# Final attention scores handed over bank by bank in two of five attention stages, in a kernel without staging copies and with reordered transposes

## Time and profile before

| | |
|---|---|
| median of 3 runs | 1514.12 us (1513.02 to 1522.76) |
| the profiled execution, its own time | 1511.47 us |
| its span, first to last instruction | 1509.8 us |
| PE busy | 1293.7 us (86%) |
| PEld busy | 855.9 us (57%) |
| DVE busy | 953.6 us (63%) |
| ACT busy | 610.6 us (40%) |
| POOL busy | 336.1 us (22%) |
| mean granted PE clock | 0.916 |

### The profile page before, as it was taken

One profiled execution on the slowest core, in us unless ns is written; L12 is line 12 of the kernel. 1 busy time (PEld: TensorE's weight loads), 2 busy tenths in 40 slices (PEclk: granted clock), 3 DMA queues, 4 the chain that ended last, 5 costly groups with the idle time before them and its releaser, 6 DMA issues. The chain is left out here.

```text
span 1509.8 us, 37147 instructions
## 1 busy us (share of the span) xinstructions
PE 1293.7 (86%) x13707; PEld 855.9 (57%) x13707; DVE 953.6 (63%) x2842; ACT 610.6 (40%) x1343; POOL 336.1 (22%) x1014
## 2 busy tenths in 40 slices
PE   3888887837858887997998887899999958999998
PEld 3777765624536773443666775435788844444443
DVE  5777737876456766998336876624777754555454
ACT  3666644651236662222344554642444421111111
POOL 1222210220033430000113331423565550000000
PEclk9999997967968997999999998756999988999999
DMA  9400000000000000000000000001000000000000
GB/s 288 104 3 3 3 2 1 2 1 1 2 1 2 3 3 1 1 1 1 1 1 2 3 3 2 1 1 57 3 3 3 3 1 0 8 15 7 7 7 15
DMA packets 26393, 21.14 MB, mean 14 GB/s; under 512 B 5936, under 2 KB 22640, under 8 KB 26224
## 3 DMA queue, kind: packets, MB, share of 16 engines
q1 hardware_dynamic: 25216, 18.67, 4.4%
q10 hardware_dynamic: 1008, 0.16, 0.1%
HBM read 16.74 MB, written 2.10 MB: 12 GB/s over the span
## 5 line engine op out<-in xcount | busy, mean ns | idle before, releaser
L311 DVE TENSOR_REDUCE neg_max<-ps 128x8 f32<-128x1024 f32 (+1 forms) x264 | 253.9, 962 | 167.6 <-PE ps L570 163.8
L559 PE MATMUL ps<-qTm,kT 32*128 32x512 f32 (+1 forms) x1056 | 247.7, 543 | 28.0 <-DVE neg_max L311 15.0
L570 PE MATMUL ps<-kT,qTm 32*128 32x128 f32 x3200 | 242.7, 287 | 0.2 <-DVE kT L332 0.2
L570 PEld LDWEIGHTS ps<-kT,qTm 32*128 32x128 f32 x3200 | 218.8, 199 | 6.2 <-issue 3.6
L476 ACT ACTIVATE probs<-ps,bias_col 128x512 f32<-128x512 f32 (+1 forms) x192 | 159.2, 829 | 123.3 <-PE ps L578 123.3
L674 PE MATMUL ps<-probs,v_wide 128*32 128x128 f32 x3200 | 116.2, 278 | 33.1 <-DVE o_sb L350 28.3
L1734 PE MATMUL ps<-kv_all,ctx_all 128*128 128x512 f32 x256 | 134.1, 606 | 5.2 <-DVE kv_all L1648 5.2
L559 PEld LDWEIGHTS ps<-qTm,kT 32*128 32x128 f32 x1056 | 83.9, 187 | 88.2 <-issue 44.9
L1672 ACT ACTIVATE kv_all<-ps,b_col 128x512 f32<-128x512 f32 x64 | 44.0, 687 | 218.8 <-PE ps L1712 218.8
L1712 PE MATMUL ps<-q_all,ctx_all 128*128 128x512 f32 x256 | 132.4, 600 | 0.0
L1648 DVE TENSOR_SCALAR kv_all<-ps,b_col 128x512 f32<-128x512 f32 x64 | 48.0, 750 | 116.5 <-PE ps L1712 116.5
(11 more groups left out here) (371 smaller groups left out, 2562.3 us busy)
## 6 DMA issues: line engine op xcount, KB each, us to landing
ctx_all<-in_ctx SPq DMA_DIRECT2D x4, 1024.0 KB, 10.5
x_all<-in_x SPq DMA_DIRECT2D x4, 512.0 KB, 6.7
out<-x_all SPq DMA_DIRECT2D x8, 256.0 KB, 2.3
ctx_all<-in_W1T SPq DMA_DIRECT2D x1, 1024.0 KB, 5.1
tap_w<-in_conv_wT SPq DMA_DIRECT2D x1, 768.0 KB
w_l<-in_w SPq DMA_DIRECT2D x2, 256.0 KB
rope<-in_c_rope SPq DMA_DIRECT2D x1, 256.0 KB
cls_mask<-in_amask SPq DMA_DIRECT2D x1, 256.0 KB
```

Source lines behind the costliest of these rows:

```text
L311: nc.vector.tensor_reduce(neg_max[:, k, H2 * u:H2 * u + H2].rearrange("p (a h) -> p a h", a=2), ps[:, 4 * u:4 * u + 2, 0:N].rearrange("p a ...
L559: nc.tensor.matmul(score_bank(g), kT[rows_of(g), k, :], qTm[rows_of(g), k, 0:N], start=not masked_scores, stop=False, skip_group_check=True)
L570: last = nc.tensor.matmul(pair_of(u, g)[:, 128 * i:128 * i + 128], qTm[rows_of(g), k, 128 * i:128 * i + 128], kT[rows_of(g), k, :], start= ...
```

## The change

In all attention stages:

- The copies `key32` and (in `post` stages) `row32` go; PE transposes from `ctx_all`, `kv_all`, `q_all` or `qk_tiles` directly.
- In `turns`, the part that signals `last_turned` comes first. In `post` stages it still holds the transpose of the maxima (bank 7) and the pick of the outputs; in the others (L0, L2: `raw`) the transpose of the maxima moves to bank 6 and to the end of the part that signals `first_turned`.
- DVE's `take_o` moves from behind `take_oT` to right behind the maximum of half 0. In raw stages it no longer waits for `nmT_ready`; there `take_qT` does.
- A half's final scores are handed over by bank in L2 and L3 (`BANKS`: 'banks'), with two semaphore counts for each half, and two exponentials of 256 columns in place of one of 512. L0, L1 and L4 stay with 'pairs'. (The third kind, 'ring', is written but no stage uses it.)

Elsewhere: the de-pooling stage gets two banks each for `ends` and `counts`, one bank for the turned rows, and PE's order becomes `ends`, `counts`, `matrix`, `turn`, `total`. The cross stage loses POOL's copy. In the experts' stage POOL waits before each of its 8 adds for `mo_choice` of that group.

```
+        BANKS = {'L0': 'pairs', 'L1': 'pairs', 'L2': 'banks', 'L3': 'banks', 'L4': 'pairs'}
+        def final_jobs(L):
+            return 2 if BANKS[L] == "pairs" else 4
+        def final_bank(L, b, g):
+            return 3 + (4 * b + (g + 2) % 4) % 3 if BANKS[L] == "ring" else 2 + g % 2
...
             def take_qT(b, k):
                 dve.wait_ge(*after("first_turned", b + 1))
+                if not post:
+                    if b < 2:
+                        dve.wait_ge(*after("early_nmT", b + 1))
+                    else:
+                        done(dve, "nmT_ready", b - 2, count)
...
                 dve.wait_ge(*after("last_turned", b + 6))
-                done(dve, "nmT_ready", b + 3, count)
+                if post:
+                    done(dve, "nmT_ready", b + 3, count)
...
                 at(2, take_max, 0)
+                at(6, take_o)
                 at(1, take_qT)
                 at(1, take_kT)
                 if post:
                     at(7, take_oT)
-                at(6, take_o)
...
             def exps(b, k, u):
+                if final_jobs(L) == 4:
+                    for g in (2 * u, 2 * u + 1):
+                        act.wait_ge(*after("scores", b * 4 + (g + 2) % 4 + 1))
+                        nc.scalar.activation(probs[:, k % 2, N * g:N * (g + 1)], ps[:, final_bank(L, b, g), 0:N],
+                                             ACT.Exp, bias=bias).then_inc(sem("probs_ready"), 1)
+                    return
...
+            def final_free(b, g):
+                if final_jobs(L) == 4:
+                    job, held = 4 * b + (g + 2) % 4, 3 if BANKS[L] == "ring" else 2
+                    if job >= held:
+                        pe.wait_ge(*after("probs_ready", job - held + 1))
...
+                    for g in s_groups:
+                        final_free(b, g)
+                        dst = ps[:, final_bank(L, b, g), 0:N]
...
+                        nc.tensor.matmul(dst, kT[rows_of(g), k, :], qTm[rows_of(g), k, 0:N],
                                          start=not masked_scores, stop=False, skip_group_check=True)
...
+                def turn_max(last):
+                    if item(3):
+                        done(pe, "nm_split", item(3)[0], count)
+                    slot = item(3)[1] if item(3) else (at_one - 2) % RING
+                    return nc.tensor.transpose(turned_max(post), nm3[:, slot, :], identb[:])
+                max_read()
+                done(pe, "o_scaled", at_one - 6, count)
+                done(pe, "pv_ready", at_one - 5, count)
+                last = turn_max(None) if post else None
+                if item(6):
...
+                    nc.tensor.transpose(ps[:, 6, 0:128], query_rows(b, k), ident[:])
+                    last = nc.tensor.transpose(ps[:, 6, 128:256], key_rows(b), ident[:])
+                if raw:
+                    last = turn_max(last)
...
+        def ends_bank(b):
+            return 4 + 3 * (b % 2)
+        def counts_bank(b):
+            return 5 - 4 * (b % 2)
...
-                wait_reuse(pe, after("dp_bound"), b, 1)
+                wait_reuse(pe, after("dp_bound"), b, 2)
...
-            steps(pe, B, [(4, matrix), (4, turn_rows(pe)), (5, total), (2, counts), (0, ends)])
+            steps(pe, B, [(0, ends), (2, counts), (4, matrix), (4, turn), (5, total)])
...
                 rows = x_all[:, bass.ts(i, 4), :]
+                pool.wait_ge(sem("mo_choice"), i + 1)
                 nc.gpsimd.tensor_tensor(rows, rows, z_all[:, bass.ts(i, 4), :], ALU.add).then_inc(sem("mo_joined"), 1)
```

More of the change, by code:

```diff
@@ L593, in mask_whole @@
             def mask_whole(b, k):
[L595 to L596 removed]
                 for a in range(2):
+                    raw_free(b, 2 + a)
                     for part in range(mask_parts):
[L599 removed]
+                        nc.tensor.matmul(ps[:, raw_bank(L, b, 2 + a), 0:N], identb[:], mask(k, part).unsqueeze(1).broadcast_to(four),
                                          start=part == 0, stop=False, skip_group_check=True)
@@ L610, in turns, with max_read @@
                 at_one = ahead[1][0] + ahead[0] - 1
+                def max_read():
+                    done(pe, "nmT_ready", at_one - 3, count)
+                    if L in BIASES and at_one in (1, 2):
+                        pe.wait_ge(*after("early_nmT", at_one))
+                early = L in BIASES and at_one < 2
+                def turn_max(last):
+                    if not (item(3) or early):
+                        return last
+                    if L in BIASES and item(1):
+                        done(pe, "bias_set", item(1)[0], count)
+                    if item(3):
[7 more added lines that the diff above has]
+                if item(6):
+                    b, k = item(6)
+                    for half in range(2):
+                        last = nc.tensor.matmul(ps[:, 7, 256 + W * half:256 + W * half + W],
+                                                pv[:, k % 2, 128 * half:128 * half + 128],
+                                                pv_pick[:, 0 if heads == 16 else 1, 0:W], start=True, stop=True)
+                if last is None:
+                    pe.sem_inc(sem("last_turned"), 1)
+                else:
+                    last.then_inc(sem("last_turned"), 1)
                 done(pe, "q_masked", at_one - 1, count)
@@ L665, in weighted @@
                 done(pe, "pv_ready", b - 1, count)
-                done(pe, "nmT_ready", b + 2, count)
+                if post:
+                    done(pe, "nmT_ready", b + 2, count)
                 done(pe, "o_scaled", b - 1, count)
@@ L669, in weighted @@
                 for half in (1, 0):
-                    pe.wait_ge(*after(ready, b * 2 + (2 - half)))
+                    each = 1 if cut_later else final_jobs(L) // 2
+                    pe.wait_ge(*after(ready, (b * 2 + (2 - half)) * each))
                     for i in range(deep):
@@ L928, in norm_b, with take_row @@
                                      scale=inv_all[:, b:b + 1]).then_inc(sem("normed"), 1)
-            steps(act, B, [(0, spread_lens), (3, norm_b), (4, take_matrix), (4, take_rows(act))])
+            def take_row(b, k):
+                act.wait_ge(*after("turned", b + 1))
+                wait_reuse(act, after("used"), b, 2)
+                nc.scalar.activation(rowT[:, k % 2, :], ps[:, 0, 0:128], ACT.Copy).then_inc(sem("rowT"), 1)
+            steps(act, B, [(0, spread_lens), (3, norm_b), (4, take_matrix), (4, take_row)])
         def depool_gpsimd(pool):
```

177 lines of the change are left out of this document (81 added, 96 removed).

## The result

The changed kernel takes 1528.84 us (median of 10 runs, 1525.79 to 1531.86) against 1514.14 for the kernel before, measured beside it: a ratio of 1.0086 with the interval 1.007 to 1.0102. By the medians it is slower by 14.7 us, by the ratio of 1.0086 by 13, where 3 us less were forecast, and it lies above the range, which ended at 1524.

The account below looks back on a forecast made before the run. Bounds were read by stage: L4 by PE, L0 and L2 by PE-ACT ping-pong, L3 by nearly full PE and DVE, de-pooling by lockstep. Terms -7 - 6 + 12 - 1 = -2 us gave 1511 us, range 1497 to 1524.

Parts of the forecast that it names:

- De-pooling, -7: De-pooling stage: second banks end the PE-DVE lockstep, a step falls from 2.00 to 1.80 us; -7 us, between -9 and 0.
- Experts, -6: Chain ahead of the experts: POOL's adds, now after the choice, stop slowing DVE's small instructions; -6 us, at worst +10.
- L3, +12: L3: new order closes a loop of 4.28 us through qT, kT, oT, above the 3.85 step; +12 us, +8 to +15.
- The clock rival: L3: PE's waiting makes the chip grant the lower clock, 5.7 us a step, +39, total 1550; chance 0.05.
- L4, 0: L4: the same loop, longer, should close some 0.4 us under the step, PE being full; 0, between -1 and +4.
- L0, "keeps pairs: 0": L0: pairs stay, turns stay inside the exponential's wait, earlier `take_o` frees nothing since ACT is the gate; 0.
- L2, -1, between -6 and +6: L2: hand-over by bank costs net +0.02 us a half, earlier `take_o` helps little; -0.03 a step, -1 us in all.
- The credit of the earlier `take_o`: L2: the earlier `take_o` removes PE's wait ahead of `weighted`, the half then held 0.05 to 0.1 us sooner.
- the other credit: L2, hand-over by bank: the first exponential starts a matmul earlier, worth about 0.05 us a half.
- L1, 0: L1: only four tiles, no step with both a maximum and a `take_o`, so no change; 0.
- The third rival: L2: two small exponentials cost their whole time, 0.96 a pair, +0.09 a half; +6 to +10, total 1519; chance 0.12.
- the others: L3's loop does not bind (1488, chance 0.12); de-pooling stays lockstepped or adds hit the path (1524, 0.12); lower clock (1550, 0.05).

Follow-up runs that it names:

- a_depool_order: Changed kernel with PE's old task order in de-pooling (matrix, turn, total, counts, ends), second banks kept: 1527.5 us, de-pooling step 1.65 us.
- b_two: Kernel before with only the de-pooling change and POOL's wait for the choice in the experts' stage: 1499.9 us.
- a_add_last: Changed kernel with DVE's add to the stream moved behind the second maximum in L1, L3 and L4: 1521.9 us, L3 step 3.84 us.
- b_act_order: Kernel before with the late wait (for PE's scores) put last in ACT's exponentials only, not in the maxima: 1523.0 us.
- b_wait_order: Kernel before with the late wait put last, behind the fulfilled one, in both exponentials and maxima: 1524.3 us.
- a_four: Changed kernel with old wait order, both banks' masks ahead of both products, L2 in pairs, and DVE's add behind the second maximum: 1499.1 us.
- a_pairs: Changed kernel with L2 and L3 handed over in pairs of banks again, one exponential of 512 columns a half: 1531.2 us.
- b_two_ahead: Kernel before with two long fulfilled waits ahead of the late one in the exponentials and the maxima: 1532.0 us.
- b_one_wait: Kernel before with the fulfilled wait left out of exponentials and maxima, so each waits for PE's scores alone: 1513.3 us.
- a_four_pe: a_four with two further long fulfilled waits in each half on PE, behind its wait for the exponential: 1511.8 us.
- a_raw_late: a_four with PE's old de-pooling order, and PE's waits for the maxima moved behind the products of the final scores: 1489.0 us.
- a_masks_first: Changed kernel with L1's mask products of both banks again ahead of both 32-row products: 1516.0 us.

## Why the prediction missed, step by step

- **De-pooling, -7.** Mechanism right, size low: -10.1, beyond its low end of -9. The loop through ACT measured 1.74 us where the estimate was 1.80, and the term that was too large is the hand-over to PE, 0.05 us for 0.12. DVE's own bound, put at 1.75 by taking off one idle time alone, is at most 1.65 (a_depool_order).
- **Experts, -6.** Right: the chain fell by 8.50 - 2.22 = 6.3 us. The adds did not come back on the path (b_two). Line 225 takes 0.19 us now that no add runs beside it, as the rule of the Trainium skill on the shared ports (page "SBUF — State Buffer", section on SBUF's two separate sides) would have it.
- **L3, +12.** The loop is right, as a_add_last shows; the close number is in part luck. The step is 4.16 to 4.18 us and not 4.28 (from the reciprocal to the second maximum 1.70 us for 1.80), which gives 9.2 us in 28 steps. The other 2.4 us of the +11.6 lie ahead of the first tile, where the granted clock was 0.50 until some 21 us into the stage, before until 11; the forecast had no term for that, and no run took it apart. The clock rival did not come: in the steady part the granted clock stayed at 1.00.
- **L4, 0.** Steps of 5.67 for 5.72, about -1.5 us, just below its low end of -1.
- **L0, "keeps pairs: 0".** Failed. The step said that nothing on the loop changed; but the loop's two hand-overs, to ACT and to DVE, had their waits exchanged. +0.12 us a step, +3.7; ACT's hand-over alone brings it (b_act_order).
- **L2, -1, between -6 and +6.** Failed, +9.2. Two terms were missing or too low: the waits, 0.09 us a step (b_wait_order), 2.8 us over 31 steps; and the net price of the hand-over by bank, 0.04 us a half instead of 0.02, 0.08 a step, 2.5 us. The credit of the earlier `take_o`, put at 0.07 a step, is 0.04 with the old waits (before 3.47, a_four 3.43) and nothing with the new ones (b_wait_order and a_pairs, both 3.56). The pair covers 0.84 us where 0.87 was said, 0.15 more than one exponential of 512 columns. The fixed cost from PSUM that the Trainium skill gives for ScalarE (page "VectorE: DVE Perf Modes", section on the TRN2 errata), 0.14 us, was nearer than my 0.18; the stage lost all the same. The credits against it were too large. By the rows the second bank's product starts 0.89 us after the start of the exponentials, before 0.83: of the 0.15 us, 0.09 is won back there, where 0.11 was said. Since a_pairs measured 0.04 us a half, the other credit, put at 0.05, was some 0.02. That the two banks' products used to run beside each other and now start one after the other would explain both; for L1 a run shows such a loss, for L2 it is only argued from the rows. About 2.4 us more came at the stage's end, where the granted clock had fallen to 0.50 and the third- and second-last steps took 4.05 and 4.07 us (before: 2.87 and 2.80); the rest, some 1.5, no run took apart.
- **L1, 0.** Failed, +9.6. The step looked only at DVE's order ("no step with both a maximum and a take_o") and not at the loop `for g in s_groups`, which by the diff now held masks and product of one bank together. The trace of before had the row that priced it, shown under L1 above: the masks of both banks, then both products in 1.13 us.
- **The third rival** (two small exponentials cost their whole time, 1519) named the right stage and the wrong reason. None of the others came.

In short: the chains of the work were right, and what the diff did to the order inside one engine's queue (waits of one instruction, matmuls of one half) was taken for nothing; in L2 the price of the hand-over by bank was too low besides. Against the forecast the stages L0, L1 and L2 came out 4.3 + 9.6 + 10.2 = 24.1 us longer, and all others together 7.2 shorter.

## What to carry to other kernels

In a loop of short hand-overs put the wait that comes last in time first, with the fulfilled ones behind it or left out, where ACT waits for PE. On PE keep at the head of a group only the waits that its first matmul needs; this gained 0.09 us a step here, for a reason that is not settled. Where matmuls on different row tiles can run side by side, issue nothing on all rows between them: a hand-over by bank that breaks such a pair gives back what it gains. And read a diff for the order of every line, also where it changes no value: some 16 of the 23 us that L0, L1 and L2 lost were such lines (3.7, 9.6 and 2.8).

## What the runs showed of the hardware

- On ACT a fulfilled wait ahead of the late one made L0's step 0.12 us longer, 0.06 a half (5.39 to 5.51, b_act_order), a second one 0.02 more a half (b_two_ahead); behind the late one, or absent, it cost nothing that the step shows (b_one_wait, 5.39).
- On PE two further fulfilled waits behind the late one made one half of L0's step 0.21 us longer and the other 0.05 shorter (a_four_pe: 2.91 and 2.65, a_four: 2.70). With the late wait alone at the head of half 1 a product started 0.06 us after the exponential's end, with the wait for the maxima ahead of it 0.15 us (a_raw_late, a_four).
- Two exponentials of 256 columns back to back cover 0.84 us (after, L2), one of 512 columns 0.69 (before).
- Two fp32 products of 512 columns on 32 rows each take 1.13 us side by side (a_masks_first) and 1.12 when one runs alone (after).
